# One TensorE program of 16 recurrence steps and 22 expert tiles: softplus through SBUF, and the feed-forward head moved among the steps

## Chip, core and metric

The kernel is one program on one core of a Trainium2 chip. The metric is the device time of one execution in microseconds (us); the lower, the better. TensorE is called PE in the profile (PEld: its weight loads), VectorE DVE, ScalarE ACT, GpSimd POOL, and SyncE's DMA queue SPq.

## The reference

```python
h = tok(x)                                     # einsum('bhid,oi,od->bho'): (4, 512, 256)
y = layernorm(h)
for _ in range(4):                             # the same weights each time
    y = mamba_block(rmsnorm(y))                # 4 batches, 512 positions, 256 features
h = h + y
h = h + ffn(layernorm(h))
# mamba_block
x_in, res = split(x @ W_in)                    # 512 + 512 features
u = silu(causal_conv4(x_in) + conv_b)
dt, Bm, Cm = split(u @ W_x)                    # 64, 16, 16
delta = softplus(dt @ W_dt + b_dt)
h_t = exp(delta_t * A) * h_(t-1) + delta_t * u_t * B_t     # 16 states for each of 512 features
y_t = sum over states of h_t * C_t;  y = (y + u * Dp) * silu(res);  return y @ W_out
# ffn, tokens as 2048 rows
e = argmax(z @ W_router)                       # one of 4 experts for each token
y = gelu(z @ W1[e] + b1[e]) @ Wo + bo + z;     return layer_norm(y)
```

## The kernel before, in words

**Steps.** One layer of one batch is a step: 16 steps, k = 0 to 15, and two more ahead (k = -2 and -1), in which the token product runs and the first steps are prepared. A step has 16 slots, one for each state s, and a slot has four places d = 0 to 3, one for each 128 features. Every engine runs its own hand-written list of work over (k, s, d); the lists meet in semaphores alone. Tables such as `WDT_AT` or `JOIN_AT` name the place after whose regular work an extra operation stands. At place (s, d) TensorE transposes delta * u * B into `b_ps[d % 2]` (`b_states`, L1316) and adds the states that are two slots old into `y_all` (`sum_states`, L1327); VectorE scans 512 positions (L1043); GpSimd multiplies two rows of four with C (`times_c`, L504, two instructions of 1024 columns a slot, `half` 0 and 1), and for states 6, 7, 10 and 12 with B (`times_b`, L495); ScalarE makes exp(delta * A) (`decay`) and the other products with B. `b_states` waits for the scan two places back; `sum_states` waits for `times_c`; `decay` waits until the hidden state of six states back is summed.

**Between the steps.** During step k the kernel prepares step k+1 (gates, dbl, delta, delta * u, its transposes) and k+2 (norm, input product, convolution), and finishes step k-1 (transpose back, output product, store to `x_dram`). The PSUM banks `bank_a` and `bank_b` serve all of this in turn, so each user waits for the reader of the one before.

**Softplus.** `to_delta` (L1247) puts dt @ W_dt into `bank_a` or `bank_b`. ScalarE makes Exp of the bank into `delta`, then Ln(1 + x) in place; VectorE takes min(max(bank, 60), delta) from the bank and from SBUF (`softplus`, L856), so that the bank is free only after that. `times_u` on GpSimd (L485) makes delta * u into `du`, which `du_turn` (L1259) transposes in slots 9 to 11. `to_delta(2)`, `back(2)` and `spread_norm` wait for softplus.

**Feed-forward head.** Layer 4 of batch b is step 12 + b. Its result is added to the h of that batch, which is turned from features to tokens first (`h_turn`, L1366; `join`, L884); then mean and variance (`head_moments`), a power of -0.5 on GpSimd (`head_root`), `head_scale` (L906), the turn of z to features (`z_turn`), the router's logits, the choice (`choose`). For two batches together `rank` and `lay_out` give each token its row in a list that is sorted by expert (at most 11 tiles of 128), `send_z` writes the tokens there by eight indirect DMAs (L539), `load_z` reads them back, and `load_w1` (L530) gathers the expert's 1 MB of weights for each tile. All of the head of batches 0 and 1 is in step 15; `send_z(0)` and the first `load_w1` follow the last step. `join(2)`, the last transposes back (`last_back`), the last output product (`last_out`, L1469 and L1472) and `head_moments` follow too, ahead of the first tile.

**Tiles.** 22 tiles, two and two: `tile_turn` (L1418) turns two tiles' tokens, `tile_copy` takes them to SBUF, `expert` (L1434) is 32 matmuls, `gelu` on ScalarE, `project_out` (L1449) 16 matmuls into `bank_a`, `keep_y` copies, `store_y` stores, `fetch_y` gathers back, and `tail_moments` and `finish` end the batch.

## Time and profile before

| | us |
|---|---|
| three runs | 2067.32, 2071.01, 2074.30; median 2071.01 |
| the profiled execution | 2073.18 |
| its span, first to last instruction | 2071.5 |
| busy in it: PE, DVE, ACT, POOL | 1850.7, 1564.5, 1464.7, 1538.3 |
| first and last scan begin | 141.4, 1832.9 |

The 1024 scans mark the steps: 64 each. Steps 0 to 13 lie between 141.4 and 1610.5 us of the span, step 14 up to 1705.0, step 15 behind it. A row of a timeline gives the start, the duration, engine, line, operation, output and inputs, and in brackets the idle time of the engine before it and what ended it; several of one kind are merged, and their shown ends overlap the next ones' starts by up to some 0.16 us on TensorE.

### The profile page before, as it was taken

The numbers are of one execution on the slowest core, as the hardware profiler recorded it, in microseconds if no ns is written. First come the engines' busy times: TensorE is split into PE (matmuls) and PEld (weight loads), VectorE is DVE, ScalarE is ACT, GpSimd is POOL, SyncE is SP. The second block draws the span as 40 slices with busy tenths as digits, with TensorE's granted clock in tenths as the row PEclk, the third lists the DMA queues.
The fourth block names the chain that finished last, engine by engine and source line by source line (L and its number), as shares of the span: only waits on it lengthen the run. The fifth ranks groups of instructions, "written<-read, shape, count | busy, mean of one in ns | idle before, by whom it ended". The sixth has DMA issues, their size and how long they took to land.

```text
span 2071.5 us, 31985 instructions
## 1 busy us (share of the span) xinstructions
PE 1850.7 (89%) x12240; PEld 1465.2 (71%) x12240; DVE 1564.5 (76%) x1703; ACT 1464.7 (71%) x2467; POOL 1538.3 (74%) x896
## 2 busy tenths in 40 slices
PE   6989899999999999999999999999898986779994
PEld 3447677777777777777777777777677775669893
DVE  1358989798989897979798988888888887752232
ACT  0268888888888888888878787878797884613231
POOL 0039898889898988888888888888989896750331
PEclk9989999999999999999999999999999998899997
DMA  7211111111111111110111111111111112152542
GB/s 248 101 51 43 52 43 61 43 62 43 62 43 62 43 61 43 48 55 34 62 41 63 41 63 42 63 41 63 42 63 41 53 52 72 62 178 85 226 144 91
DMA packets 46394, 144.27 MB, mean 70 GB/s; under 512 B 7009, under 2 KB 18529, under 8 KB 42914
## 3 DMA queue, kind: packets, MB, share of 16 engines
q1 hardware_dynamic: 41538, 114.97, 16.2%
q0 software_dynamic: 4704, 27.27, 3.7%
q8 instruction: 97, 1.59, 0.3%
q14 instruction: 55, 0.45, 0.1%
HBM read 119.67 MB, written 22.54 MB: 69 GB/s over the span
## 4 chain that ended last, share of the span: by engine, by line
PE 52%; DVE 19%; issue 12%; ACT 12%; POOL 2%; DMA 2%; SPq 0%; DVEq 0%; POOLq 0%; ACTq 0%
PE b_ps L1316 12%; DVE hid L1043 10%; PE y_all L1327 9%; ACT dub_t L694 6%; ACT hid L681 5%; DVE u L851 4%; PE bank_b L1199 3%; PE bank_a L1449 3%; PE y_all L1118 3%; PE bank_b L1214 3%; PE bank_a L1223 3%; PE b_ps L1434 2%; PE y_all L1434 2%; PE bank_a L1247 2%; PE bank_a L1214 2%
## 5 line engine op out<-in xcount | busy, mean ns | idle before, releaser
L1043 DVE TENSOR_TENSOR_SCAN hid<-hid,b_ps 128x512 f32<-128x512 f32 x1024 | 1218.3, 1210 | 243.2 <-PE b_ps L1316 222.8
L504 POOL TENSOR_TENSOR hid<-hid,c_rep 128x1024 f32<-128x1024 f32 x512 | 1210.3, 2383 | 221.5 <-DVE hid L1043 221.5
L1316 PEld LDWEIGHTS b_ps<-ident,dub_t 128*128 128x128 f32 x4096 | 488.7, 143 | 375.5 <-issue 231.1
L1316 PE MATMUL b_ps<-ident,dub_t 128*128 128x128 f32 x4096 | 634.9, 278 | 78.9 <-DVE hid L1043 74.9
L681 ACT ACTIVATE hid<-delta,neg_a 128x512 f32<-128x512 f32 x1024 | 652.7, 710 | 0.2
L1327 PE MATMUL y_all<-ident,hid 128*128 128x128 f32 x4096 | 620.6, 275 | 3.8 <-POOL hid L504 3.8
L694 ACT ACTIVATE dub_t<-du_t,b_t 128x512 f32<-128x512 f32 x768 | 490.2, 711 | 54.8 <-PE b_ps L1316 53.1
L1327 PEld LDWEIGHTS y_all<-ident,hid 128*128 128x128 f32 x4096 | 485.7, 143 | 4.8 <-POOL hid L504 4.8
L495 POOL TENSOR_SCALAR dub_t<-du_t,b_t 128x512 f32<-128x512 f32 x256 | 173.8, 707 | 0.0
L1199 PE MATMUL bank_b<-xn,w_in_sb 128*128 128x512 f32 x256 | 134.5, 612 | 15.6 <-DVE xn L838 12.5
L851 DVE SCALAR_TENSOR_TENSOR u<-bank_b,conv_w_sb,u 128x511 f32<-128x511 f32 (+2 forms) x192 | 139.4, 726 | 0.7
L659 ACT ACTIVATE du_t<-bank_a 128x512 f32<-128x512 f32 x64 | 38.0, 593 | 90.0 <-PE bank_a L1259 90.0
L1296 PE MATMUL bank_a<-y_d,w_out_sb 128*128 128x512 f32 x192 | 98.3, 594 | 0.0
L485 POOL TENSOR_TENSOR du<-delta,u 128x1024 f32<-128x1024 f32 x32 | 75.7, 2366 | 29.2 <-DVE delta L856 29.2
L992 DVE COPY hid<-bank_a 128x512 f32<-128x512 f32 x11 | 7.6, 692 | 95.6 <-PE bank_a L1449 95.6
L1449 PE MATMUL bank_a<-dub_t,hid 128*128 128x256 f32 x352 | 79.7, 380 | 0.0
L1118 PE MATMUL y_all<-hid,dub_t 128*128 128x512 f32 x128 | 62.5, 631 | 14.7 <-DMA hid<-x_t 14.7
L1449 PEld LDWEIGHTS bank_a<-dub_t,hid 128*128 128x128 f32 x352 | 65.3, 190 | 8.0
L669 ACT ACTIVATE x_out<-bank_a 128x512 f32<-128x512 f32 x30 | 17.7, 589 | 73.6 <-PE bank_a L1296 46.1
L1334 PE MATMUL y_all<-diag_skip,u 128*128 128x128 f32 x512 | 67.6, 275 | 0.0
L1214 PE MATMUL bank_b<-w_in_sb,xn 128*128 128x512 f32 x128 | 66.3, 602 | 1.1 <-DVE u L851 1.1
L1214 PE MATMUL bank_a<-w_in_sb,xn 128*128 128x512 f32 x128 | 66.6, 605 | 0.1
(210 smaller groups left out, 1613.1 us busy)
## 6 DMA issues: line engine op xcount, KB each, us to landing
c_rep<-bc_dram SPq DMA_DIRECT2D x128, 512.0 KB, 3.6
hid<-x_t SPq DMA_DIRECT2D x4, 2048.0 KB, 8.8
xt<-x_dram SPq DMA_DIRECT2D x15, 512.0 KB, 3.6
x_dram<-x_out SPq DMA_DIRECT2D x15, 512.0 KB, 2.9
z_dram<-du SPq DMA_DIRECT2D x2, 1408.0 KB, 18.9
y_dram<-hid SPq DMA_DIRECT2D x22, 128.0 KB, 2.0
h_dram<-hid SPq DMA_DIRECT2D x4, 512.0 KB, 3.9
x_dram<-hid SPq DMA_DIRECT2D x3, 512.0 KB, 2.7
```

The source lines that it names most:

```text
L495: nc.gpsimd.tensor_scalar(dub_t[:, i % DUB, tc, :], du_t[:, k % 2, tc, :], b_t[:, k % 2, tc, s:s + 1], 1.0, ALU.mult, ALU.mult).then_inc(d ...
L504: nc.gpsimd.tensor_tensor(part, part, c_rep[:, n % 2, s % GROUP, :].unsqueeze(1) .broadcast_to([P, HALF, SEQ]), ALU.mult).then_inc(hc_read ...
L681: nc.scalar.activation(hid[:, i % RING, d, :], delta[:, k % 2, d, :], ACT.Exp, scale=neg_a[:, d, s:s + 1]).then_inc(decay_ready, 1)
L694: nc.scalar.activation(dub_t[:, i % DUB, tc, :], du_t[:, k % 2, tc, :], ACT.Copy, scale=b_t[:, k % 2, tc, s:s + 1]).then_inc(dub_act, 1)
L851: nc.vector.scalar_tensor_tensor(u[:, k % 2, m, t:], bank_b[:, 0:SEQ - t], conv_w_sb[:, m, w:w + 1], u[:, k % 2, m, t:], ALU.mult, ALU.add ...
L1043: nc.vector.tensor_tensor_scan(hid[:, i % RING, d, :], hid[:, i % RING, d, :], b_ps[d % 2][:, :], 0.0, ALU.mult, ALU.add)\
L1118: last = nc.tensor.matmul(y_all[:, DC * (b % 2) + m, :], wc[:, kc, m * P:(m + 1) * P], hid[:, 2 * (b % 2) + kc // NI, kc % NI, :], start=k ...
L1199: ins = nc.tensor.matmul(bank_b[:, :], w_in_sb[:, c, m * P:(m + 1) * P], xn[:, c, :], start=c == 0, stop=c == DC - 1)
L1214: ins = nc.tensor.matmul((bank_a if tc % 2 == 0 else bank_b)[:, :], xn[:, c, tc * P:(tc + 1) * P], w_in_sb[:, c, INNER:], start=c == 0, st ...
L1316: last = nc.tensor.transpose(b_ps[d % 2][:, c * P:(c + 1) * P], dub_t[:, i % DUB, c, d * P:(d + 1) * P], ident[:, :])
L1327: last = nc.tensor.matmul(y_ps[d][:, c * P:(c + 1) * P], hid[:, i % RING, d, c * P:(c + 1) * P], ident[:, :], start=s == 0 and c == 0, sto ...
L1449: last = nc.tensor.matmul(bank_a[:, (t % 2) * D:(t % 2 + 1) * D], inter[t % 2][:, c, :], wo_sb[:, c // 2, (c % 2) * D:(c % 2 + 1) * D], st ...
```

## The change

- **Softplus.** ScalarE copies each bank to `delta` (`delta_copy`, semaphore `delta_in`), makes Exp of two rows of four (1024 columns) into `du`, and Ln in place there. VectorE takes the minimum from `delta` and `du`, both in SBUF, 1024 columns at a time, twice a step. The users of the banks wait for `delta_in` instead of `delta_ready`. `to_delta(2)` and `(3)` are one place earlier, `spread_norm` and `normalize` too; `times_u` on GpSimd stands behind `times_c(7, 0)` and `times_c(8, 0)`, not (6, 1) and (7, 1).
- **Head.** Batch 0: loads, turns, joins, moments, root and scale in step 14, the logits in slot 0 and choose in slot 2 of step 15. Batch 1: slots 4 to 9 of step 15. `rank(0)` in slot 10, `lay_out(0)` in slot 11, `send_z(0)` in slots 12 and 13, three `load_w1` in slots 11, 14 and 15.
- **Last batch.** The first tile comes right behind the last sums; `last_back`, `last_out`, `h_turn(2)` and the heads of batches 2 and 3 stand among the first seven tiles. `send_z(1)` follows `load_w1(11)`.
- **Tile turns.** Six turns for each group of 11 tiles, the last with one tile, so that no turn holds tiles of both.

The diff, cut; each batch's scratch, the waits and the banks of the moved parts follow from this.

```diff
+TURNS = [tuple(range(t, min(t + 2, TILES))) for t in range(0, TILES, 2)]
+TURNS += [tuple(t + TILES for t in turn) for turn in TURNS]
+TURN_OF = {t: p for p, turn in enumerate(TURNS) for t in turn}
...
                         if k == STEPS - 1:
-                            load_x_tokens(0)
-                            load_h(1)
                             load_x_tokens(1)
...
+                            if k == STEPS - 2 and g == 4:
+                                load_h(0)
+                                load_x_tokens(0)
                             if k == STEPS - 2 and g == 5:
-                                load_h(0)
+                                load_h(1)
...
                     load_wo()
+                    load_z(0)
                     store_x(STEPS - 2)
                     load_x_tokens(2)
-                    load_z(0)
                     for p in range(3):
...
-                        else:
-                            pool.wait_ge(z_zeroed, 2 * 16)
...
+                    def send_z(g, c):
+                        if c == 0:
+                            pool.wait_ge(z_zeroed, 2 * 16)
+                            pool.wait_ge(z_ready, TC * PAIR * (g + 1))
+                            pool.wait_ge(pos_ready, g + 1)
+                        nc.gpsimd.indirect_dma_start(out=z_dram[g], out_offset=bass.IndirectOffsetOnAxis(ap=pos[:, g, c:c + 1], axis=0),
+                                                     in_=f_z[PAIR * g + c // TC][:, c % TC, :], in_offset=None).then_inc(z_out[g], 16)
...
+                    LOAD_W1_AT = {(11, 1): 0, (14, 0): 1, (15, 0): 2}
+                    SEND_Z_AT = {(12, 0): (0, 1), (12, 1): (2, 3), (13, 0): (4, 5), (13, 1): (6, 7)}
...
-                                if live(k + 1) and (s, half) == (6, 1):
+                                if live(k + 1) and (s, half) == (7, 0):
                                     times_u(k + 1, 0)
-                                if live(k + 1) and (s, half) == (7, 1):
+                                if live(k + 1) and (s, half) == (8, 0):
                                     times_u(k + 1, 1)
...
-                                if k == STEPS - 1 and (s, half) == (3, 0):
+                                if (k, s, half) == (STEPS - 2, 11, 1):
                                     head_root(0)
-                                if k == STEPS - 1 and (s, half) == (10, 1):
+                                if (k, s, half) == (STEPS - 1, 6, 0):
                                     head_root(1)
-
-                    load_w1(0)
-                    send_z(0)
-                    for t in range(1, 5):
+                                if k == STEPS - 1 and (s, half) in LOAD_W1_AT:
+                                    load_w1(LOAD_W1_AT[s, half])
+                                if k == STEPS - 1 and (s, half) in SEND_Z_AT:
+                                    for c in SEND_Z_AT[s, half]:
+                                        send_z(0, c)
+
+                    for t in range(3, 6):
                         load_w1(t)
                     head_root(2)
+                    load_w1(6)
                     head_root(3)
-                    for t in range(5, 8):
+                    for t in range(7, 12):
                         load_w1(t)
-                    send_z(1)
-                    for t in range(8, 16):
+                    for c in range(CH):
+                        send_z(1, c)
+                    for t in range(12, 18):
                         load_w1(t)
                     fetch_y(0)
                     fetch_y(1)
-                    load_w1(16)
-                    load_w1(17)
+                    load_w1(18)
                     tail_root(0)
-                    load_w1(18)
+                    load_w1(19)
...
-                    def delta_exp(k, d):
+                    def delta_copy(k, d):
                         act.wait_ge(wdt_done, NI * k + d + 1)
-                        nc.scalar.activation(delta[:, k % 2, d, :], (bank_a if d % 2 == 0 else bank_b)[:, :], ACT.Exp)\
-                            .then_inc(exp_ready, 1)
-
-                    def delta_log(k, d):
-                        act.wait_ge(exp_ready, NI * k + d + 1)
-                        nc.scalar.activation(delta[:, k % 2, d, :], delta[:, k % 2, d, :], ACT.Ln, bias=1.0).then_inc(log_ready, 1)
+                        nc.scalar.activation(delta[:, k % 2, d, :], (bank_a if d % 2 == 0 else bank_b)[:, :], ACT.Copy).then_inc(delta_in, 1)
+
+                    def delta_exp(k, half):
+                        rows = slice(half * HALF, (half + 1) * HALF)
+                        act.wait_ge(delta_in, NI * k + HALF * (half + 1))
+                        if k:
+                            act.wait_ge(dut_done, TC * k)
+                        else:
+                            act.wait_ge(z_zeroed, 2 * 16)
+                        nc.scalar.activation(du[:, rows, :], delta[:, k % 2, rows, :], ACT.Exp).then_inc(exp_ready, 1)
+
+                    def delta_log(k, half):
+                        rows = slice(half * HALF, (half + 1) * HALF)
+                        act.wait_ge(exp_ready, 2 * k + half + 1)
+                        nc.scalar.activation(du[:, rows, :], du[:, rows, :], ACT.Ln, bias=1.0).then_inc(log_ready, 1)
...
-                                delta_exp(k + 1, 0)
-                                delta_exp(k + 1, 1)
-                                delta_log(k + 1, 0)
-                                delta_log(k + 1, 1)
+                                for half in range(2):
+                                    delta_copy(k + 1, 2 * half)
+                                    delta_copy(k + 1, 2 * half + 1)
+                                    delta_exp(k + 1, half)
+                                    delta_log(k + 1, half)
...
-                        last_y_copy(dc)
+                    gelu(0)
+                    last_y_copy(0)
+                    last_y_copy(1)
+                    gelu(1)
+                    last_y_copy(2)
+                    last_y_copy(3)
+                    gelu(2)
                     last_x_copy(0)
                     last_x_copy(1)
-                    for t in range(ALL_TILES):
+                    gelu(3)
+                    z_t_copy(2, 0)
+                    z_t_copy(2, 1)
+                    gelu(4)
+                    z_t_copy(3, 0)
+                    z_t_copy(3, 1)
+                    for t in range(5, ALL_TILES):
                         gelu(t)
-                        if t in (0, 2):
-                            for m in range(DC):
-                                z_t_copy(2 + t // 2, m)
 
                 @block.vector
...
-                    def softplus(k, d):
-                        dve.wait_ge(log_ready, NI * k + d + 1)
-                        nc.vector.scalar_tensor_tensor(delta[:, k % 2, d, :], (bank_a if d % 2 == 0 else bank_b)[:, :], 60.0,
-                                                       delta[:, k % 2, d, :], ALU.max, ALU.min).then_inc(delta_ready, 1)
+                    def softplus(k, half):
+                        rows = slice(half * HALF, (half + 1) * HALF)
+                        dve.wait_ge(log_ready, 2 * k + half + 1)
+                        nc.vector.scalar_tensor_tensor(delta[:, k % 2, rows, :], delta[:, k % 2, rows, :], 60.0, du[:, rows, :],
+                                                       ALU.max, ALU.min).then_inc(delta_ready, HALF)
...
-                    SOFTPLUS_AT = {(7, 0): 0, (7, 1): 1, (8, 0): 2, (8, 1): 3}
+                    SOFTPLUS_AT = {(7, 1): 0, (7, 3): 1}
...
-                    JOIN_AT = {(1, 0): (0, 0), (2, 1): (0, 1), (9, 0): (1, 0), (9, 3): (1, 1)}
-                    MOMENTS_AT = {(2, 3): 0, (10, 1): 1}
-                    SCALE_AT = {(4, 2): 0, (11, 3): 1}
-                    CHOOSE_AT = {(8, 0): 0, (14, 2): 1}
+                    JOIN_AT = {(STEPS - 2, 9, 2): (0, 0), (STEPS - 2, 10, 3): (0, 1), (STEPS - 1, 4, 2): (1, 0), (STEPS - 1, 5, 2): (1, 1)}
+                    MOMENTS_AT = {(STEPS - 2, 11, 0): 0, (STEPS - 1, 5, 3): 1}
+                    SCALE_AT = {(STEPS - 2, 13, 0): 0, (STEPS - 1, 7, 0): 1}
+                    CHOOSE_AT = {(STEPS - 1, 2, 1): 0, (STEPS - 1, 9, 3): 1}
...
+                    tile_copy(0)
                     pick_bias(0)
-                    join(2, 0)
-                    join(2, 1)
-                    head_moments(2)
-                    head_scale(2)
-                    tile_copy(0)
-                    head_moments(3)
                     for t in range(ALL_TILES):
-                        if t % 2 == 0 and t + 2 < ALL_TILES:
-                            tile_copy(t // 2 + 1)
-                        if t == 0:
+                        if t in (turn[0] for turn in TURNS) and TURN_OF[t] + 1 < len(TURNS):
+                            tile_copy(TURN_OF[t] + 1)
+                        if t == 2:
+                            join(2, 0)
+                            join(2, 1)
+                            head_moments(2)
+                            head_moments(3)
+                        if t == 3:
+                            head_scale(2)
                             head_scale(3)
-                        if t == 1:
+                        if t == 5:
                             choose(2)
-                        if t == 3:
+                        if t == 6:
                             choose(3)
-                        if t == 4:
...
-                            pe.wait_ge(delta_ready, NI * k + d - 1)
+                            pe.wait_ge(delta_in, NI * k + d - 1)
...
-                    WDT_AT = {(6, 1): 0, (6, 2): 1, (7, 1): 2, (7, 2): 3}
+                    WDT_AT = {(6, 1): 0, (6, 2): 1, (7, 0): 2, (7, 1): 3}
...
-                    H_TURN_AT = {(0, 2): (0, 0), (1, 2): (0, 1), (8, 2): (1, 0), (9, 2): (1, 1)}
-                    Z_TURN_AT = {(5, 3): (0, 0), (6, 3): (0, 1), (12, 2): (1, 0), (13, 1): (1, 1)}
-                    LOGITS_AT = {(7, 2): 0, (14, 0): 1}
+                    H_TURN_AT = {(STEPS - 2, 9, 0): (0, 0), (STEPS - 2, 10, 1): (0, 1), (STEPS - 1, 4, 0): (1, 0), (STEPS - 1, 5, 0): (1, 1)}
+                    Z_TURN_AT = {(STEPS - 2, 14, 0): (0, 0), (STEPS - 2, 15, 3): (0, 1), (STEPS - 1, 7, 3): (1, 0), (STEPS - 1, 8, 1): (1, 1)}
+                    LOGITS_AT = {(STEPS - 1, 0, 3): 0, (STEPS - 1, 9, 2): 1}
...
-                                if live(k + 2) and at == (8, 2):
+                                if live(k + 2) and at == (8, 1):
...
+                                if (k, s, d) == (STEPS - 1, 10, 3):
                                     rank(0)
...
-                    for dc in range(NI):
-                        last_back(dc)
-                    h_turn(2, 0)
-                    h_turn(2, 1)
-                    last_out(0)
-                    last_out(1)
                     tile_turn(0)
                     expert(0)
+                    last_back(0)
+                    last_back(1)
                     for t in range(ALL_TILES):
-                        if t % 2 == 0 and t + 2 < ALL_TILES:
-                            tile_turn(t // 2 + 1)
+                        if t in (turn[0] for turn in TURNS) and TURN_OF[t] + 1 < len(TURNS):
+                            tile_turn(TURN_OF[t] + 1)
+                        if t == 5:
+                            z_turn(3, 1)
                         if t + 1 < ALL_TILES:
                             expert(t + 1)
-                        if t in (0, 2):
-                            z_turn(2 + t // 2, 0)
-                            z_turn(2 + t // 2, 1)
-                        if t in (1, 3):
-                            logits(2 + t // 2)
+                        if t == 0:
+                            last_back(2)
+                            last_back(3)
+                        if t == 1:
+                            last_out(0)
+                            last_out(1)
+                        if t == 2:
+                            h_turn(2, 0)
+                            h_turn(2, 1)
+                        if t == 3:
+                            z_turn(2, 0)
+                            z_turn(2, 1)
                         if t == 4:
+                            logits(2)
+                            z_turn(3, 0)
+                        if t == 5:
+                            logits(3)
+                        if t == 6:
                             rank(1)
```

## Rows read from the trace of the kernel before

**Rows 1.** Busy us (count) by window: PE, PEld, DVE, ACT, POOL; clock, DMA, GB/s.
```profile
141.40:1610.50 1469.10, 1358.39 (x9304) 1066.96 (x9305) 1270.50 (x1272) 1219.68 (x1981) 1283.61 (x714) 0.99 0.15 51
...
1610.50:1705.00 94.50, 87.62 (x644) 73.42 (x643) 80.42 (x76) 82.78 (x137) 87.89 (x50) 1.00 0.17 57
...
1705.00:1836.60 131.60, 97.56 (x691) 89.00 (x689) 100.40 (x120) 66.19 (x108) 92.51 (x52) 0.87 0.18 61
...
1836.60:1865.90 29.30, 16.70 (x84) 13.72 (x84) 10.43 (x36) 3.96 (x7) 13.96 (x14) 0.86 0.82 297
...
1865.90:2041.80 175.90, 172.19 (x1162) 161.78 (x1162) 44.98 (x110) 53.33 (x181) 37.92 (x36) 0.97 0.40 144
...
2041.80:2071.50 29.70, 0.00 (x0) 0.00 (x0) 14.61 (x33) 0.00 (x0) 9.92 (x10) 0.56 0.24 80
```

**Rows 2.** Timeline of VectorE (DVE), step 5, slots 8 and 9.
```profile
716.20 1.22 DVE L1043 TENSOR_TENSOR_SCAN hid<-hid,b_ps 128x512 f32<-128x512 f32 x1 [1.25 <-PE b_ps L1316]
...
726.95 1.21 DVE L1043 TENSOR_TENSOR_SCAN hid<-hid,b_ps 128x512 f32<-128x512 f32 x1
```

**Rows 3.** Timeline of TensorE (PE), step 5, slots 7 to 9.
```profile
708.63 1.12 PE L1247 MATMUL bank_a<-dbl,w_dt_sb 128*128 128x512 f32 x2 [0.60 <-DVE delta L856]
...
715.00 0.66 PE L1281 MATMUL bank_a<-ident,yg_t 128*128 128x128 f32 x4 [1.76 <-DVE delta L856]
...
715.50 0.60 PE L1316 MATMUL b_ps<-ident,dub_t 128*128 128x128 f32 x4
...
715.93 0.60 PE L1327 MATMUL y_all<-ident,hid 128*128 128x128 f32 x4
...
725.27 0.60 PE L1259 MATMUL bank_a<-ident,du 128*128 128x128 f32 x4
```

**Rows 4.** Timeline of GpSimd (POOL), step 5, slots 6 to 9.
```profile
705.02 4.72 POOL L504 TENSOR_TENSOR hid<-hid,c_rep 128x1024 f32<-128x1024 f32 x2
...
718.09 2.37 POOL L485 TENSOR_TENSOR du<-delta,u 128x1024 f32<-128x1024 f32 x1 [0.70 <-DVE delta L856]
...
720.43 2.70 POOL L495 TENSOR_SCALAR dub_t<-du_t,b_t 128x512 f32<-128x512 f32 x4
```

**Rows 5.** Timeline, VectorE instructions with two SBUF inputs, and a GpSimd product.
```profile
1834.22 2.36 POOL L504 TENSOR_TENSOR hid<-hid,c_rep 128x1024 f32<-128x1024 f32 x1 [3.77 <-DVE hid L1043]
...
1834.48 2.12 DVE L943 TENSOR_TENSOR_SCAN until<-ones,used 128x4 f32<-128x4 f32 x1
...
1912.92 0.17 DVE L943 TENSOR_TENSOR_SCAN until<-ones,used 128x4 f32<-128x4 f32 x1
...
1944.94 1.22 DVE L998 TENSOR_TENSOR hid<-hid,rows 128x1024 f32<-128x1024 f32 x1
```

**Rows 6.** Groups of GpSimd's instructions by line, step 15.
```profile
L509 POOL TENSOR_TENSOR f_norm<-f_norm,half_power 128x4 f32<-128x4 f32 x2 | 2.1, 1026 | 0.0
```

**Rows 7.** Timeline, waits in step 15.
```profile
1720.24 2.54 DVE L1043 TENSOR_TENSOR_SCAN hid<-hid,b_ps 128x512 f32<-128x512 f32 x2 [10.80 <-PE b_ps L1316]
...
1751.02 0.66 PE L1316 MATMUL b_ps<-ident,dub_t 128*128 128x128 f32 x4 [4.39 <-DVE hid L1043]
...
1752.22 1.06 PE L1281 MATMUL bank_b<-ident,yg_t 128*128 128x128 f32 x4
```

**Rows 8.** Timeline, from the last product to the first expert tile.
```profile
1848.15 0.97 POOL L539 DMA_INDIRECT z_dram<-du,pos  x1 [0.30 <-issue]
...
1864.15 0.98 PE L1418 MATMUL bank_b<-ident,xt 128*128 128x128 f32 x4 [3.12 <-DMA xt<-z_dram]
...
1865.91 6.30 PE L1434 MATMUL b_ps<-hid,delta 128*128 128x128 f32 x32 [0.78 <-DVE hid L986]
```

**Rows 9.** Timeline, last_out and the tile loop.
```profile
1856.97 1.89 PE L1469 MATMUL y_all<-w_out_sb,y_d 128*128 128x256 f32 x8
...
1923.29 3.74 PE L1434 MATMUL y_all<-hid,gate_t 128*128 128x128 f32 x32
...
1933.74 6.49 PE L1434 MATMUL b_ps<-hid,delta 128*128 128x128 f32 x32 [3.26 <-issue]
```

195 lines of the change are left out of this document (96 added, 99 removed).

## The prediction

> **What bounds the kernel now.** I read the busy times by stage first, cut at the first scan of a step [rows 1]. Fourteen steps of the recurrence take 1469.1 us, 104.9 each; TensorE is busy 92% of that, GpSimd 87%, VectorE 86%, ScalarE 83%. No engine is far ahead: a slot (one state, four scans) is set by the hand-written order. Step 14 takes 94.5 us with GpSimd busy 87.9, so GpSimd bounds it. Step 15, up to the end of GpSimd's last product, takes 131.6 with nothing above 101. Then 29.3 us pass before the first expert tile, the tile loop takes 175.9 with TensorE busy 172.2, and 29.7 follow it.
>
> The timeline of one regular step shows what softplus costs there. TensorE waits 0.60 us for a bank that softplus still reads, and 1.76 before a transpose back [rows 3]; VectorE's scan (8,1) starts 1.25 late for it [rows 2]. At the opening of step 15 a scan starts 10.80 us late [rows 7]: TensorE sits in h_turn(0, 0), whose tokens are loaded only after store_x(13). After the last scan the chain is send_z, its landing, load_z, the first tile_turn: the first expert matmul comes 29.3 us after GpSimd's end, on a slow TensorE [rows 8].
>
> **Softplus, before GpSimd is counted.** ScalarE gets four copies out of PSUM for four Exp, two Exp and two Ln of 1024 columns for four Ln of 512: some 1.8 us more a step, in an engine that idles 17% [rows 1]; I cost it at nothing. VectorE does two instructions of 1024 for four of 512. The row for a sum of two 1024-wide SBUF inputs is 1.22 [rows 5], so 2.3 against 2.3. TensorE's waits of 0.60 and 1.76 go, since a bank is free after its copy. TensorE would reach du_turn(0) in slot (9,2) at about 722.7 in place of 725.27.
>
> **Softplus, with GpSimd.** There it meets the moved products. times_u stands behind times_c(7,0) and times_c(8,0) now. In the old order the second du was ready at 720.46 [rows 4]. In the new one GpSimd ends times_c(6,1) at 709.74 and then has in a row times_c(7,0), times_u(0), times_c(7,1), the four times_b of state 10, times_c(8,0), times_u(1): five of 2.36 and one of 2.70, 14.5 us, so 724.2 at the earliest. du_turn(0), which stands in front of the transposes for scan (9,3), waits for that. Scan (9,3) started at 726.95; with du ready at 724.2 it would start 0.44 (one group of TensorE [rows 3]), 0.7 (from a group's start to its scan, 715.50 to 716.20 [rows 2, 3]) and 0.1 (a semaphore) later, 725.45: a gain of 1.5 us a step. That is the bound from below.
>
> The new softplus reads both inputs from SBUF, and such an instruction does not run beside a GpSimd product. The 4-column scan of lay_out took 2.12 us and ended with GpSimd's product at 1836.6; the same one took 0.17 with GpSimd idle [rows 5]. So a softplus waits for what is left of a product (0 to 2.36). What it costs GpSimd no row shows: at least 0, at most its own 1.1 us (1.22 less the overlap of one instruction with the next). Rows for the exclusion have VectorE waiting for a whole product, so I take the whole 1.1 for the other way round too. Two of them put du at 726.4, in either order of who goes first, since GpSimd's sum is the same. TensorE then waits 3.7 us at (9,2); scan (9,3) starts at 727.6, 0.6 later than before. After a wait of 4.39 in step 15 TensorE's next but one group took 1.06 in place of 0.60 [rows 7]: the lower of its two clock levels. Two groups before the scan put it at 728.6, 1.7 later. I take the middle, 1.1 us a step slower, and for the upper bound 2.6 (one more wait of a full product by VectorE, partly hidden). Fourteen steps: +15.4, bounds -21 and +36.
>
> The Trainium skill, "SBUF — State Buffer", section "Who interferes with whom", says that a VectorE instruction with two SBUF inputs contends with a GpSimd instruction that reads SBUF, one input going through the read interface that they share. It speaks against this edit: by it the 1.1 us count in full, without it the gain of 1.5 a step would stand. The 2.12 beside 0.17 agrees with it.
>
> **Step 14.** GpSimd bounds it: plus two softplus (2.2), a head_root (1.0 [rows 6]), and what small contention head_scale brings, about 0.8: +4.0 (bounds 2 and 9, if VectorE's head_moments and head_scale, or the wait for the root behind times_c(11,1), show too). The two h_turn, two z_turn and the joins fit into 6.9 us of TensorE's idle time and 14 of VectorE's.
>
> **Step 15.** The 10.80 goes: h_turn(0, ·) is in step 14, and h_turn(1, 0) comes four slots after the store it needs. The head work of batch 0 goes but for choose. GpSimd takes on send_z(0), eight issues of 0.97 with 0.30 between, and three load_w1 of the same size [rows 8]: 14.0 us that lay behind the step. Its work is then 32 products of 2.36, 75.5, four times_b of 2.70, 10.8, one head_root, 14.0: 101.3. To that come waits: it keeps its two slots of lag over the step's start; head_scale(1) behind head_root(1), choose(1) and above all lay_out(0), whose two-input instructions each wait for a product, hold VectorE until GpSimd runs dry. I add 14.7, so 116 (bounds 108 and 124) against 131.6: -15.6.
>
> **From the last product to the first tile.** send_z(0) ends in slot 13, two slots and two load_w1 before the last product (some 12 us); from the last issue to the first tile_turn it was 16.0 [rows 8], with four load_w1 beside the transfer. So the first tile's tokens are there a little before TensorE has done the last sums and out_x. sum_states, out_x, tile_turn, tile_copy: 5.2 us against 29.3, -24.1 (bounds -25 and -16, if load_z is late). last_back and last_out wait in the loop now.
>
> **Tile loop.** TensorE bounds it, so what enters counts: four last_back of 0.44, 1.8; two last_out, in four parts of 1.89 [rows 9] and the turns behind them, 8; h_turn(2, ·), 0.9. What leaves: the wait of 3.26 before expert(8), whose load_w1 stood behind send_z(1), and the slow first tile, 6.3 us of matmuls for 3.7 [rows 8, 9]. In the new order send_z(1) stands behind load_w1(11), and tile_turn(6) needs its tokens some 27 us after rank(1), against 17 of DVE, send_z and load_z; I count no wait. 10.7 - 3.3 - 2.6 = +4.8 (bounds 2 and 12). The last turn has one tile and one store: -0.6 after the loop.
>
> **Sum** against the profiled execution, 2073.18 us (span 2071.5, 1.7 around it): +15.4 + 4.0 - 15.6 - 24.1 + 4.8 - 0.6 = -16.1, so 2057.1. That execution lies 2.2 above the median of the runs, 2071.01: 2055 us.
>
> **Rivals.** (1) *The reordering's gain survives*: GpSimd isn't held by softplus, or is held while it has nothing to do. For it: GpSimd idles 13% of the fourteen steps, and no row shows it held. Against: it has no idle time between 709.7 and du. 14 x (-1.5 to 0) in place of +15.4: 2018 to 2040, say 2030. Chance 0.20. (2) *The tail stalls*: load_z lands late or the interleaved last_back, last_out and the z copies leave TensorE waiting for ScalarE and VectorE in the first five tiles. Price up to 9 and 7, say 12: 2067. For it: send and load took 16.0 us; against: ScalarE is busy 53 of 176 there. Chance 0.09. (3) *Slower than before*: the softplus in SBUF is the worse part of the change. Both of them find a product just begun and wait 2.36, and du comes later by as much. All the rest gives -31.5; so 14 steps must lose 2.25 each to cancel it, and 2.7 each (+37.8) to be over 0.3% slower. 2.5 to 3.5 each give 2075 to 2089. Chance 0.07; between 1.8 and 2.7 each, no measurable change, 2065 to 2077, chance 0.09. The rest, 0.55, is my forecast, whose own range is 2043 to 2065.
>
> A measurement tells 0.3%, 6 us, from no change: faster is under 2064.8. Faster: 0.55 + 0.20 = 0.75; same 0.09 + 0.09 = 0.18; slower 0.07. The range leaves out the lower half of rival 1 and the slower case: 2030 to 2070.
>
> **What the new profile would show.** Softplus rows of 1024 columns of 1.2 to 3.5 us, ending with a GpSimd product, and GpSimd products of 3.4 beside them; TensorE waiting for du at the transposes to du_t; regular steps of 105 to 107 us. No scan over 5 us late at the opening of step 15; GpSimd's last product some 116 us after the step's first scan; the first expert matmul about 5 us behind it. If softplus rows are all 1.2 and steps under 104, rival 1 holds. The prediction falls if a step is off by over 1 us, or if lay_out(0) beside GpSimd costs step 15 more than 10.

## The result and the profile after

The changed kernel takes 2075.61 us, median of ten runs, against 2068.12 for the kernel before, ten runs too: ratio 1.003, 95% interval 1.0017 to 1.0044. It is a little slower, where 2055 with a range of 2030 to 2070 was forecast. One of the ten took 2548.41 at a granted clock of 0.71 where the others have 0.96; the ratio is of the other nine, whose median is 2074.78. The profiled execution took 2074.78 us, span 2073.0. The windows, cut at the same events as in [rows 1]: steps 0 to 13, step 14, step 15 up to the end of GpSimd's last product, the stretch to the first expert matmul, and the tile loop.

```profile
137.70:1620.10 1482.40, 1374.68 (x9303) 1089.26 (x9304) 1294.38 (x1243) 1249.05 (x1984) 1300.53 (x714) 0.97 0.15 50
1620.10:1724.00 103.90, 91.43 (x658) 77.92 (x657) 90.57 (x89) 84.83 (x136) 92.16 (x51) 0.97 0.18 62
1724.00:1851.50 127.50, 94.14 (x678) 86.64 (x675) 100.69 (x114) 66.34 (x109) 100.65 (x61) 0.87 0.26 91
1851.50:1855.60 4.10, 3.30 (x21) 2.81 (x21) 2.07 (x6) 0.60 (x1) 1.92 (x2) 1.00 0.86 314
1855.60:2043.90 188.30, 181.96 (x1226) 169.26 (x1226) 51.71 (x132) 56.15 (x187) 36.42 (x37) 0.98 0.42 150
```

Set beside [rows 1] and the forecast's terms, us:

| stretch | before | after | difference | forecast |
|---|---|---|---|---|
| up to the first scan | 141.4 | 137.7 | -3.7 | 0 |
| steps 0 to 13 | 1469.1 | 1482.4 | +13.3 | +15.4 |
| step 14 | 94.5 | 103.9 | +9.4 | +4.0 |
| step 15 | 131.6 | 127.5 | -4.1 | -15.6 |
| to the first expert | 29.3 | 4.1 | -25.2 | -24.1 |
| tile loop | 175.9 | 188.3 | +12.4 | +4.8 |
| behind it | 29.7 | 29.1 | -0.6 | -0.6 |
| sum | 2071.5 | 2073.0 | +1.5 | -16.1 |

**Regular steps.** The timeline of step 5, VectorE first, then GpSimd, answers to [rows 2, 4]. Columns: start, duration, engine, line, operation; in brackets the idle time ahead.

```profile
714.47 1.22 DVE L1084 TENSOR_TENSOR_SCAN hid<-hid,b_ps 128x512 f32<-128x512 f32 x1 [0.28 <-PE b_ps L1355]
715.61 3.76 DVE L892 SCALAR_TENSOR_TENSOR delta<-delta,du 128x1024 f32<-128x1024 f32 x1
719.29 2.32 DVE L1084 TENSOR_TENSOR_SCAN hid<-hid,b_ps 128x512 f32<-128x512 f32 x2
721.53 1.36 DVE L892 SCALAR_TENSOR_TENSOR delta<-delta,du 128x1024 f32<-128x1024 f32 x1
```
```profile
711.21 7.07 POOL L513 TENSOR_TENSOR hid<-hid,c_rep 128x1024 f32<-128x1024 f32 x3
719.44 2.36 POOL L494 TENSOR_TENSOR du<-delta,u 128x1024 f32<-128x1024 f32 x1 [1.16 <-DVE delta L892]
721.76 3.35 POOL L513 TENSOR_TENSOR hid<-hid,c_rep 128x1024 f32<-128x1024 f32 x1
```

The first softplus takes 3.76 us in place of 1.2: it doesn't run until GpSimd's row of three products has ended at 718.28. GpSimd, whose next work is the du product of that softplus, then idles 1.16. The second softplus gets in first (1.36), and the product that starts at 721.76 takes 3.35 in place of 2.36. So the exclusion acts both ways, as the forecast assumed without a row for the second.

Four of the fourteen steps (0, 2, 8 and 12) are of another kind: both softplus go first, in 1.2 to 1.4 us, and GpSimd is held twice. GpSimd, then TensorE, in step 2:

```profile
398.35 3.28 POOL L513 TENSOR_TENSOR hid<-hid,c_rep 128x1024 f32<-128x1024 f32 x1 [0.23 <-DVE hid L1084]
401.59 3.37 POOL L494 TENSOR_TENSOR du<-delta,u 128x1024 f32<-128x1024 f32 x1
```
```profile
414.67 0.66 PE L1300 MATMUL bank_a<-ident,du 128*128 128x128 f32 x4 [3.18 <-POOL du L494]
```

These steps, with the short softplus, are no faster: 107.2, 107.1, 107.1 and 105.6 us, where the ten with a long one take 105.0 to 106.2. The second du is ready 63.2 to 64.8 us behind the step's first scan in either kind. Where softplus waited, TensorE has already waited 3.2 us for the scans in slot 7, and waits at most 1.15 for du; where it did not, TensorE waits 3.2 to 3.5 for du. Over the 14 steps:

```profile
L892 DVE SCALAR_TENSOR_TENSOR delta<-delta,du 128x1024 f32<-128x1024 f32 x28 | 61.0, 2179 | 0.0
```

Mean 2.18 where 1.2 is the undisturbed duration. The Trainium skill, "SBUF — State Buffer", "Who interferes with whom", says that for the pair of ports it is the order of issue that decides who is blocked. The second softplus, 1.36, agrees: it starts at 721.53, ahead of the product that it holds. The first doesn't fit by the starts that the profile gives: it starts at 715.61, and the third product of the row (three in 7.07 us from 711.21) about 0.3 later, and still that product goes first.

**Step 15.** VectorE, then GpSimd, at head_moments(1):

```profile
1763.59 0.38 DVE L932 BATCH_NORM_AGGREGATE moments<-stats 128x2 f32<-128x6 f32 x4
1764.01 5.30 DVE L934 TENSOR_SCALAR f_norm<-moments 128x4 f32<-128x4 f32 x1
1769.22 2.32 DVE L1084 TENSOR_TENSOR_SCAN hid<-hid,b_ps 128x512 f32<-128x512 f32 x2
```
```profile
1764.59 4.69 POOL L513 TENSOR_TENSOR hid<-hid,c_rep 128x1024 f32<-128x1024 f32 x2
1771.68 2.36 POOL L513 TENSOR_TENSOR hid<-hid,c_rep 128x1024 f32<-128x1024 f32 x1 [2.40 <-DVE hid L1084]
```

The addition of 1e-5 on four columns, one input, took 5.30 us: it ends with the second of two products that follow one another, both of which start after it, and the scans stand behind it. It took 0.73 and 0.72 in step 15 of the kernel before. The slot took 12.1 us. Thirty us later the first comparison of choose(1) takes 2.37 for 8 columns, beside one product. The next four small instructions take 0.62 to 0.65 each, beside four `times_b` that follow one another without a gap; here VectorE was let in behind each of them. TensorE idles 5.06:

```profile
1794.22 2.37 DVE L955 TENSOR_TENSOR top<-logit 128x8 f32<-128x8 f32 x1
1796.63 0.62 DVE L957 TENSOR_TENSOR best<-top 128x4 f32<-128x4 f32 x1
...
1796.55 2.70 POOL L504 TENSOR_SCALAR dub_t<-du_t,b_t 128x512 f32<-128x512 f32 x4
...
1800.93 1.12 PE L1355 MATMUL b_ps<-ident,dub_t 128*128 128x128 f32 x4 [5.06 <-DVE hid L1084]
```

The group behind that wait takes 1.12 where one at the full clock takes 0.60: again the lower of the two levels. What GpSimd waited for in step 15, in the list of waits:

```profile
POOL hid L513 <- DVE hid L1084: 24.4, 15, 3.6
```

### The profile page after: what moved, and what is told of

It reads as the page before. It is cut to its first block, busy times and chain, and to the rows that moved or that the text cites. A ratio compares the mean times of both kernels' runs of the same rounds, so it can differ in the third digit from the quotient of the medians.

```text
span 2073.0 us, 32022 instructions
## 1 busy us (share of the span) xinstructions
PE 1860.4 (90%) x12240; PEld 1484.5 (72%) x12240; DVE 1596.7 (77%) x1673; ACT 1496.0 (72%) x2467; POOL 1554.0 (75%) x896
## 3 DMA queue, kind: packets, MB, share of 16 engines
q1 hardware_dynamic: 41538, 114.97, 16.1%
## 4 chain that ended last, share of the span: by engine, by line
PE 53%; DVE 15%; ACT 11%; issue 10%; POOL 10%; DMA 1%; SPq 0%; DVEq 0%; POOLq 0%; ACTq 0%
PE b_ps L1355 13%; PE y_all L1366 10%; DVE hid L1084 8%; ACT dub_t L719 5%; POOL hid L513 5%; ACT hid L706 5%; PE bank_a L1484 4%; DVE u L886 3%; PE y_all L1159 3%; PE bank_b L1255 3%; PE bank_a L1264 2%; PE bank_b L1240 2%; POOL du L494 2%; PE b_ps L1468 2%; PE y_all L1468 2%
## 5 line engine op out<-in xcount | busy, mean ns | idle before, releaser
L513 POOL TENSOR_TENSOR hid<-hid,c_rep 128x1024 f32<-128x1024 f32 x512 | 1225.9, 2412 | 213.8 <-DVE hid L1084 213.3
L1355 PEld LDWEIGHTS b_ps<-ident,dub_t 128*128 128x128 f32 x4096 | 497.9, 145 | 421.9 <-issue 221.2
L1355 PE MATMUL b_ps<-ident,dub_t 128*128 128x128 f32 x4096 | 646.1, 282 | 124.3 <-DVE hid L1084 117.3
L1366 PE MATMUL y_all<-ident,hid 128*128 128x128 f32 x4096 | 631.5, 278 | 8.7 <-POOL hid L513 8.7
L1366 PEld LDWEIGHTS y_all<-ident,hid 128*128 128x128 f32 x4096 | 495.0, 145 | 10.2 <-POOL hid L513 10.2
L1033 DVE COPY hid<-bank_a 128x512 f32<-128x512 f32 (+1 forms) x12 | 7.8, 647 | 119.6 <-PE bank_a L1484 90.1
L694 ACT ACTIVATE x_out<-bank_a 128x512 f32<-128x512 f32 x30 | 17.7, 588 | 81.8 <-PE bank_a L1335 46.1
L1159 PE MATMUL y_all<-hid,dub_t 128*128 128x512 f32 x128 | 62.8, 634 | 15.4 <-DMA hid<-x_t 15.4
L892 DVE SCALAR_TENSOR_TENSOR delta<-delta,du 128x1024 f32<-128x1024 f32 x32 | 68.9, 2155 | 8.4 <-ACT du L680 8.4
## 6 DMA issues: line engine op xcount, KB each, us to landing
z_dram<-du SPq DMA_DIRECT2D x2, 1408.0 KB, 19.6
```

The source lines that it names most:

```text
L513: nc.gpsimd.tensor_tensor(part, part, c_rep[:, n % 2, s % GROUP, :].unsqueeze(1) .broadcast_to([P, HALF, SEQ]), ALU.mult).then_inc(hc_read ...
L1159: last = nc.tensor.matmul(y_all[:, DC * (b % 2) + m, :], wc[:, kc, m * P:(m + 1) * P], hid[:, 2 * (b % 2) + kc // NI, kc % NI, :], start=k ...
L1355: last = nc.tensor.transpose(b_ps[d % 2][:, c * P:(c + 1) * P], dub_t[:, i % DUB, c, d * P:(d + 1) * P], ident[:, :])
L1366: last = nc.tensor.matmul(y_ps[d][:, c * P:(c + 1) * P], hid[:, i % RING, d, c * P:(c + 1) * P], ident[:, :], start=s == 0 and c == 0, sto ...
```

## Experiments

"Steps" is the stretch of steps 0 to 13. Runs 1 to 4, 5 to 8, 9 to 12 and 13 to 15 each shared a chip and the executions of the kernel before on it, median 2061.5, 2063.3, 2061.2 and 2060.2 us; the ratio is to these, and it is what compares runs of different groups.

**1. The softplus part alone.** `delta_copy`, Exp and Ln of 1024 columns, the new `softplus`, WDT_AT, the places of the norm and of `times_u`; all else as before.

> The kernel before with the softplus part of the change alone; the head, the dispatch and the tail stay where they were. Theory 1 (the SBUF softplus contends with GpSimd's products and loses in every step): the 13.3 us that the steps 0 to 13 lost stand here whole, some 1 to 2 more for step 14, so 2068 + 11 to 17, 2079 to 2085 us; regular steps of 105 to 107. Theory 3 (the moves of the head, the dispatch and the tail are what costs): within 3 us of before, 2065 to 2071.

2077.3 us, ratio 1.0065 (1.0039 to 1.009), steps 1481.0 against 1469.1. Theory 1 holds: the softplus part by itself costs 13 to 16 us. In the waits of TensorE, those for softplus are gone, and this one has come:

```profile
PE bank_a L1264 <- POOL du L484: 33.2, 14, 3.4
```

It is 2.4 us a step in the mean, at the first transpose of du.

**2. All but the softplus part.**

> The changed kernel with the old softplus and its old places (from PSUM, four of 512 columns); the head, the dispatch and the tail are moved as in the change. Theory 1: the stages from step 14 on keep their differences, less two softplus (step 14 +7, step 15 -4, last product to first tile -25, tile loop +12), and the steps are back: before - 8 to - 16, 2052 to 2060 us. Theory 3: 2070 or more.

2060.4 us, ratio 0.9985 (0.997 to 0.9999). The second half of theory 1 failed: the moved head, dispatch and tail gain some 3 us, not 8 to 16. The ratios of the two parts multiply to 1.005, and the whole change has 1.003. Step 14 is 103.6 without the new softplus, step 15 127.6, the loop 184.2.

**3. The second du product early**, on run 1:

```diff
-                                if live(k + 1) and (s, half) == (8, 0):
+                                if live(k + 1) and (s, half) == (7, 1):
                                     times_u(k + 1, 1)
```

> The softplus part alone with GpSimd's second du product at its old place, behind times_c(7,1) and ahead of the four times_b of state 10. Theory 2 (the late place of the du products in GpSimd's order is what the steps lose): TensorE's wait for du goes, 1 us a step or more back, at least 14 us under the softplus part alone. Theory 1 (contention: VectorE waits a product, GpSimd is held): du comes earlier by 2.7 us, but a softplus still meets a product, so at most 0.5 us a step back, within 7 us of the softplus part alone.

2051.36 us, ratio 0.9951 (0.9922 to 0.998): 26 us under run 1, and faster than before. Theory 2 holds: the softplus still meets the products, but TensorE never waits for du. Theory 1 as I had it, contention alone, fell. The two kinds of steps are there again, and now the short softplus gives the short step. Step 2 took 102.2, step 3 104.8:

```profile
390.52 1.38 DVE L861 SCALAR_TENSOR_TENSOR delta<-delta,du 128x1024 f32<-128x1024 f32 x1
...
394.06 1.20 DVE L861 SCALAR_TENSOR_TENSOR delta<-delta,du 128x1024 f32<-128x1024 f32 x1
...
492.84 3.74 DVE L861 SCALAR_TENSOR_TENSOR delta<-delta,du 128x1024 f32<-128x1024 f32 x1
...
498.74 1.35 DVE L861 SCALAR_TENSOR_TENSOR delta<-delta,du 128x1024 f32<-128x1024 f32 x1
```

In step 2 both softplus go first, in step 3 the first one waits a product. The six executions lie between 2036 and 2061; the profiled one, 2036, has eleven of fourteen steps in which no softplus took over 1.5 us.

**4. No minimum on VectorE**, on run 1. ScalarE's Ln writes `delta`, and the bound against overflow of Exp is left out.

> The softplus part alone without VectorE's two instructions: ScalarE's Ln writes delta itself, which leaves out the bound that keeps softplus right where Exp overflows. Everything else, GpSimd's order too, is that of the softplus part alone. Theory 1: with the contention, 2.4 us of VectorE and the late start of the scans behind it gone, a step is at or under 104 us, 1.5 to 3 less than the softplus part alone: 20 to 42 us under it, under the kernel before. Theory 2 (order and lateness of du): du still ends some 14.5 us after times_c(6,1); at most 5 us under the softplus part alone.

2032.8 us, ratio 0.985 (0.9822 to 0.9878), steps 1446.2, most of them 102.8. That is theory 1's way, and a little beyond its 20 to 42: without contention and VectorE's 2.4 us a step, and with du as late in GpSimd's order as before, it is 44 us less than run 1. TensorE still waits for du, 20.1 us in 14 times.

**5. Both**: no minimum, du early.

> The softplus part alone without VectorE's two instructions (the bound against overflow is left out) and with the second du product at its old place: fourth corner of the square contention by order. If the two prices add up (order 2 us a step, as with contention 26 us over 14 steps), this is 2033 - 26 = 2007 us. If the late du costs only because GpSimd is held on the way to it, the order is worth much less without contention: TensorE's wait in slot 9 (8.1 in place of 6.3) is what is left, 1.5 us a step, 2010 to 2015; if nothing, 2033.

2022.64 us, ratio 0.9807 (0.9786 to 0.9829), steps 1430.7, nine of the fourteen 101.7 to 101.8. The square, medians in us:

| | du late | du early |
|---|---|---|
| softplus on VectorE from SBUF | 2077.3 | 2051.4 |
| no minimum | 2032.8 | 2022.6 |

The two don't add up: the place of du is worth 26 us with the minimum, 10 without, and 2022.6 lies between the 2010 to 2015 and the 2033 of the expectation. The minimum costs 44 and 29. VectorE's own time in it is 34 (28 times 1.2 us), more than the 29, so part of it must be hidden there. How much of the rest is exclusion and how much own time the square does not tell.

**6. The dispatch behind step 15**, on run 2: the eight `send_z(0)` and three `load_w1` again follow the last product.

> The old softplus, the head moved as in the change, but send_z(0) and the first three load_w1 stand behind GpSimd's last product as before. What the dispatch inside step 15 is worth by itself. If the 14 us of issues in front of the last products only moved from behind them (theory: the gain is the landing and load_z that they now run beside, 10 to 12 us), this is 10 to 14 us over the run with the head moved and the old softplus. Rival: GpSimd idles 24 us in step 15, so the issues fit into idle time and their whole 25 us behind the step are gained: 20 us or more over it.

2069.34 us, ratio 1.0032 (1.002 to 1.0044), 0.0047 or 10 us over run 2, at the lower end of the first theory. The windows show how: step 15 falls from 127.6 to 115.6, so the 14 us of issues cost 12.0 inside the step. GpSimd's idle time doesn't take them in: it waits 24.7 us for scans there with the issues, and 25.9 without. The stretch behind the step grows from 4.1 to 26.0.

**7. The small addition on GpSimd**, on run 2:

```diff
-                        nc.vector.tensor_scalar(f_norm[:, own, :], moments[:, own, :, 1], 1e-5, None, ALU.add).then_inc(f_ve_ready, 1)
...
+                        pool.wait_ge(bn_ready, 2 * TC * (b + 1))
+                        nc.gpsimd.tensor_scalar(f_norm[:, own, :], moments[:, own, :, 1], 1e-5, None, ALU.add).then_inc(f_ve_ready, 1)
```

> The old softplus, everything else moved as in the change, and the addition of 1e-5 on 4 columns in head_moments is made by GpSimd just ahead of its root, in place of VectorE. Theory: this small VectorE instruction took 4.00 us in step 14 and 5.26 in step 15 because it waits for GpSimd's products, and scans stand behind it; with it gone step 14 and step 15 lose 4 to 8 us together, 2052 to 2057 on the chip where the head alone took 2060. Rival: GpSimd's own sum bounds both steps, the wait is hidden: within 2 us of the head alone.

2060.58 us, ratio 0.9988 (0.9974 to 1.0002): nothing, as the rival says, but not for its reason. The 4.00 and 5.26 us are gone, and head_scale, which was cheap as long as GpSimd had run dry before it, takes them. The next run has the same code in place; VectorE, then GpSimd, in its step 14:

```profile
1669.71 5.46 DVE L944 TENSOR_SCALAR du<-w_in_sb,moments,f_norm 128x256 f32<-128x256 f32 x4
```
```profile
1668.32 0.24 POOL L519 TENSOR_SCALAR f_norm<-moments 128x4 f32<-128x4 f32 x1
...
1669.65 4.72 POOL L513 TENSOR_TENSOR hid<-hid,c_rep 128x1024 f32<-128x1024 f32 x2
```

Four instructions of 0.40 take 5.46: two of them wait a product each, the second of these until GpSimd's row ends at 1674.37, and two run behind it. GpSimd does the addition in 0.24.

**8. The whole change with runs 3 and 7 in it.**

> The whole change with two repairs: the second du product at its old place (behind times_c(7,1)), and the addition of 1e-5 in head_moments on GpSimd. If the repairs act as they did one by one (order -26 us on the softplus part, small addition -4 to -8): 2068 - 26 - 6, 2035 to 2050 us, 10 to 25 under the kernel before, the fastest exact kernel so far. Rival: in the step with the head in it GpSimd takes the gain back: 2055 or more.

2041.66 us, ratio 0.9907 (0.9882 to 0.9932): inside the expectation.

**9. The whole change, only the du product moved.**

> The whole change with one line's place altered: times_u(1), the second du product, at its old place behind times_c(7,1) and ahead of the four times_b of state 10. If the late du is what the contention turns into lost time: the 26 us that it gave on the softplus part alone, so some 0.8 to 1.3% under the kernel before where the change was 0.3% over it, ratio 0.987 to 0.992. Rival (the gain is given back in steps 14 and 15): ratio 0.995 or more.

2049.86 us, ratio 0.9949 (0.9928 to 0.997), between the two expectations. One place in GpSimd's order turns a change that loses 0.3% into one that gains 0.5%. In its profiled execution eight of the fourteen steps have a softplus of 3.74 us or more.

**10. head_scale of batches 0 and 1 on ScalarE**, on run 8.

> The change with the two repairs, and head_scale of batches 0 and 1 moved from VectorE to ScalarE (GpSimd prepares minus mean times root on 4 columns; z_turn and logits of batch 0 come some slots later). Theory: what moved from the small addition to head_scale in that run (two instructions of 2.42 to 2.46 us in place of 0.40 in step 14, one in step 15, and slots of 10.8 and 12 to 13 us) is again VectorE waiting for whole GpSimd products; with it gone step 14 gets to 98 to 101 us from 105.0 and step 15 loses 3 to 5: 7 to 11 us under the change with two repairs. Rival (GpSimd's sum bounds step 14): within 3 us of it.

2040.17 us, ratio 0.9912 (0.9881 to 0.9942), no different from run 8 in the median, where 7 to 11 less was expected. In the profiles step 14 is 96.9 against 105.0, as the theory has it, and step 15 stays at 125.7 against 125.6. The steps differ the other way by 11.0 (1460.1 and 1449.1, by which kind of step came). With four executions of one and six of the other, spread over 11 and 15 us, the medians can't show the 8 us; that they are hidden by the kinds of steps is argued.

**11. last_back and last_out ahead of tile 0**, on run 8.

> The change with the two repairs, but last_back and last_out of the last batch all before tile 0, as in the kernel before (h_turn(2) stays in the loop). The tile loop falls by what the interleave put into it, some 10 us (tile 1 took 14.8 us where the old order has 8.8), and the stretch from the last product to the first tile grows by the same work plus its round trips to ScalarE: 4.1 becomes 16 to 18. Net 2 to 5 us slower than the change with the two repairs if the round trips count; the same if not.

2047.77 us, ratio 0.9937 (0.9911 to 0.9962); the interval overlaps that of run 8. By the windows the stretch behind step 15 takes 16.9 and the loop 169.7, together 186.6, against 4.1 and 184.9, 189.0, with a wait of 3.34 us in it for the tokens of tile_turn(6), of which more below. What the interleave is worth stays open; it is little.

**12. The two softplus side by side**, on run 8, behind scans (7,2) and (7,3).

> The change with the two repairs, and the two softplus instructions moved to stand behind scans (7,2) and (7,3). If each softplus meets a just-begun product by chance of its place: slot 7 takes 9.8 us in fewer or more of the 14 steps, the fast step stays 102.2, and the median moves by at most 10 us either way. If the exclusion costs GpSimd 1 us for each softplus whatever its place, the fast step is no shorter than 102.2; a fast step under 101.5 would say that the place alone makes the cost.

2064.25 us, ratio 1.0019 (1.0003 to 1.0036), 22 us over run 8, more than expected. All fourteen steps have both softplus long, 1.88 to 2.72 and 2.46 or 2.47: the slot takes 9.5 us or more in each. So the place decides which kind of step comes.

**13 and 14. All the head's work off VectorE that meets a product**: with run 10, choose for batches 0 and 1 keeps a maximum and a comparison on VectorE, both reading the logits from PSUM; five small steps go to GpSimd. Run 13 has the old softplus, run 14 the new one with du early.

> The head, dispatch and tail of the change with the old softplus, and all of the head's small VectorE work that meets GpSimd's products taken off VectorE: the addition of 1e-5 on GpSimd, head_scale of batches 0 and 1 on ScalarE, and of choose for batches 0 and 1 only a maximum and a comparison left, both read from PSUM, the rest on GpSimd. If contention is what kept the moved head from its gain: step 14 at 95 to 98 us (head alone: 103.6), step 15 at 117 to 122 (head alone: 127.6), so 12 to 17 us under the head alone, ratio to the kernel before 0.990 to 0.993. Rival (GpSimd's sum of products and issues bounds step 15): step 15 stays over 125, ratio 0.994 or more.

2045.19 us, ratio 0.9923 (0.9905 to 0.9941).

> The whole change with all repairs: the second du product at its old place, and the head's small work off VectorE as in the run with the old softplus. If the two repairs are independent: the change with two repairs and head_scale on ScalarE (ratio 0.991) less 5 to 8 us in step 15 for choose, so ratio 0.986 to 0.989, the fastest exact kernel. Rival (step 15 bound by GpSimd): 0.991 again.

2034.81 us, ratio 0.9878 (0.9856 to 0.99), the fastest kernel that computes all of the reference, 1.2% under the kernel before. Step 15 is 120.9 and 119.9, both inside the expectations. Against run 2 the slot with the addition falls from 12.1 to 6.8 in run 13 and that of choose(1) from 12.8 to 7.2, but slots 7 and 8 together grow from 11.7 to 20.3. The longest slot left there, 12.9 us in run 14, is that of lay_out(0), the one small chain that was not moved. VectorE, then GpSimd, run 14:

```profile
1767.18 6.50 DVE L1029 TENSOR_TENSOR_SCAN until<-ones,used 128x4 f32<-128x4 f32 x1
```
```profile
1766.65 7.01 POOL L515 TENSOR_TENSOR hid<-hid,c_rep 128x1024 f32<-128x1024 f32 x3
```

Four columns wait out three products; in the changed kernel the same instruction met one, and took 2.12. TensorE idles 8.20 behind it.

**15. The kernel before, a second profile.**

> The kernel before once more, for a second profile. If its 3.26 us without an instruction before expert(8), and the clock lapses of five of fourteen steps, belong to the one execution: the tile loop takes 170 us in place of 175.9, and other steps have the lapse.

2056.94 us on its chip, where the median was 2060.2. Its windows, step 14 to the loop:

```profile
1609.40:1703.90 94.50, 87.65 (x644) 73.44 (x642) 80.46 (x77) 82.79 (x137) 87.90 (x50) 1.00 0.17 57
1703.90:1831.30 127.40, 95.55 (x691) 86.49 (x689) 97.72 (x120) 66.15 (x108) 92.32 (x52) 0.89 0.19 63
1831.30:1857.70 26.40, 16.57 (x85) 13.70 (x85) 10.54 (x37) 3.96 (x7) 13.98 (x15) 0.87 0.81 294
1857.70:2025.60 167.90, 167.02 (x1162) 156.62 (x1162) 44.95 (x109) 53.06 (x181) 36.76 (x36) 1.00 0.43 156
```

The loop took 167.9 where 170 was expected. Beside [rows 1]: step 14 is the same, step 15 4.2 shorter, the stretch behind it 2.9, the loop 8.0, and the wait of 3.26 us in [rows 9] is not there.

## Why the prediction was wrong

**What failed: the waits of step 15.** "I add 14.7, so 116": step 15 was to take 101.3 us of GpSimd's work and 14.7 of waits. The work is right: GpSimd is busy 100.65 in that window. The waits are 127.5 - 100.65 = 26.9, 12.2 more than forecast, and 24.4 of them are for scans. I knew the mechanism and named head_scale(1), choose(1) and lay_out(0), but left out head_moments(1), whose last instruction is the dearest (5.30), and costed a wait as one product. A VectorE instruction that meets GpSimd's products can wait for one, two or three (2.12, 5.30, 6.50). What decides how many is not shown: the long ones end where GpSimd has nothing more ready, yet in choose(1) VectorE was let in between instructions that stood ready. The closing sentence gave lay_out(0) beside GpSimd as the danger; it cost 2.12. This term was off by 11.5 us. Runs 13 and 14 show that such meetings make the larger part of it: with choose, head_scale and the addition off VectorE the step falls from 127.6 to 120.9 and 119.9, though lay_out(0) now takes 6.46 and 6.50. The rest, up to 116, is not separated.

**Step 14**, +4.0 with a bound of 9, came to +9.4. I put "what small contention head_scale brings" at 0.8 and the addition at nothing. Run 2 shows the head there costing 9.1 without the new softplus (103.6 against 94.5), with 4.00 us for the addition; run 13, with nothing of it on VectorE, has 95.7. So some 8 of the 9 come with the head's small work on VectorE, contention as far as the rows show; run 13 also has the two z_turn of batch 0 a few slots later, which is not separated. Run 7 shows why one repair is not enough: the wait goes to the next such instruction.

**The tile loop**, +4.8, came to +12.4. What enters was costed right: run 6 has 180.7, and the old order in run 1 170.0, so 10.7, as forecast. What was to leave was not the kernel's: the 3.26 us wait before expert(8) stood in one execution. Of six profiles with the old tail (before twice, runs 1, 3, 4, 5) only that one has a hole of over 1 us.

"I count no wait" before tile_turn(6) failed too, though not in the changed kernel's own profile. The tokens were to be there 17 us behind rank(1), and needed at 27. In seven of the eleven profiles with the new tail (runs 2, 7, 8, 9, 10, 12, 14) TensorE waits 1.3 to 3.3 us for them:

```profile
1918.62 1.09 PE L1451 MATMUL bank_b<-ident,hid 128*128 128x128 f32 x4 [3.34 <-DMA hid<-z_dram]
```

This is run 8. In the seven the first load_z(1) lands 25.5 to 27.6 us behind the scan of lay_out(1), in the other four 21.5 to 22.3, in the two profiles of the kernel before 17.7 and 19.6; where nothing is late, as in run 13, tile_turn(6) comes 24.2 behind that scan. The loop of run 2, with a wait of 2.13 and the next expert at the lower clock level (6.60 for 3.73), is 5.0 longer than that of run 13.

The changed kernel's two holes are of another kind. Near 1940 and 1981 us TensorE and its weight loads stand in the midst of an expert's 32 matmuls, with nothing named that they wait for; the two experts and the projections behind them take 9 more than undisturbed ones. The cause is open; no run was aimed at it.

**The steps**, +15.4 for +13.3: right in size, and run 1 alone has +11.9 in the profile and some 13 to 16 in the runs. Both prices held: VectorE waits a product (3.76) and GpSimd is held 1 us (3.35 for 2.36). The path held as well: the second du was to be ready at 726.4, which is 63.6 us behind the first scan of its step, and it came at 63.2 to 64.8 in either order. That the steps with a long softplus lose about as much as those with a short one rests on TensorE's 3.2 us for the scans in slot 7, which the forecast had in its upper bound alone; there the size is partly luck. What I did not see is how much of it hung on the place of du. I let two softplus put du at 726.4 "in either order", in the new order of GpSimd only; run 3 takes 26 us off by letting du pass the four `times_b`. Rival 1 (chance 0.20) did not come: GpSimd was held. The reason against it, "no idle time between 709.7 and du", was not exact: in step 5 GpSimd idles 1.16 there, waiting for softplus.

**From the last product to the first tile**, -24.1 for -25.2, and the late scan of 10.80 at the opening of step 15, which is gone (the first slot takes 7.0 for 16.6): right.

**The base.** The medians differ by +7.5 where the terms said -16.1. Of these 23.6 us, 17.6 are the terms; 5.1 is that the profiled execution lay above the ten-run median (I took off 2.2, against a median of three), 0.8 that the one after lies below its own. And executions differ most where I took my gains from: run 15 has step 15, the stretch and the loop 15.1 us shorter in sum.

**The rivals.** Rival 3, slower than before, was put on softplus: 14 steps losing 2.7 each, chance 0.07. The steps lost 0.95 each. The sign turned instead because the two stages with the head in them gained 16.9 us less than forecast, both beyond their bounds (127.5 with 124 for step 15, 9.4 with 9 for step 14), and the loop 7.6 less; I had no rival for either. Rival 2, load_z late, was meant for the first tiles, which came 4.1 us behind the last product; it is met at tile_turn(6) instead.

## What to carry to other kernels

Where GpSimd works back to back, list every VectorE instruction, however small, that could stand in its way, and price each as a range: from the rest of one GpSimd instruction to the whole row of them that is ready at that point. What stands behind it on VectorE pays. Removing one such instruction can move the wait to the next, so take the whole chain away: to ScalarE, to GpSimd itself, or to operands in PSUM. When an edit makes two engines contend, put the product that the rest waits for ahead of the work that can wait: here one place in GpSimd's order was worth 26 us. And take a stall off a forecast only when a second profile of the same kernel has it.

## What the runs showed of the hardware

- An addition on 128x4 took 5.30 us, a scan on 128x4 6.50: they ended with the second and third of GpSimd's products in a row, which were started after (5.30) or just before them. Four small instructions of choose(1) took only 0.62 to 0.65 beside a gapless row of four `times_b`. The reduction ahead of the scan of lay_out was not held: 0.19 beside a product.
- With the softplus behind scans (7,1) and (7,3) of regular steps, one took 1.2 to 1.4 us or, in most cases where GpSimd was first, 3.7 to 3.8, and up to 4.5 in a few. With du early the step took 102.2 to 104.0 without a long one and 104.1 to 106.4 with it. Executions of run 3 spread over 25 us (2036 to 2061), where the kernel before spreads over 10 to 16.
- A step in which slot 6 falls to the lower clock level and takes 8.0 us in place of 6.3 is followed by a cheap slot 7: all 30 such slots in the profiles of the changed kernel and runs 1, 3, 8, 9, 10, 11 and 14 stand ahead of one of 7.1 us. In run 12, where the softplus stand elsewhere, three such slots stand ahead of one of 9.7. In run 9 the steps with the lapse took 103.2 to 104.0, and those that met a product 104.5 to 106.2. The lapse costs 1.7, and slot 7 is 2.7 shorter behind it (7.1 for 9.8).
